# Short runs of indirect transfers, with a wait for a turned block between them, in a routed-experts kernel

## What is computed

```python
def ffn(x, router_w, w1, w2):                     # x: (4, 512, 128), 8 experts, hidden 512
    xf = x.reshape(-1, d)
    probs = softmax(xf @ router_w.T, axis=-1)
    topv, topi = top_k(probs, 2)
    topv = topv / (topv.sum(axis=-1, keepdims=True) + 1e-09)
    cw = (one_hot(topi, e) * topv[..., None]).sum(axis=1)
    h = gelu(einsum('td,edh->teh', xf, w1), approximate=False)
    y = einsum('teh,ehd->ted', h, w2)
    return einsum('te,ted->td', cw, y).reshape(b, s, d)

x = x + 0.5 * ffn(layernorm(x), router_w, w1, w2)
x = x + attention(layernorm(x), Qw, Kw, Vw)       # causal, one head of 128
x = x + 0.5 * ffn(layernorm(x), router_w, w1, w2)
```

## Time and profile before

| | |
|---|---|
| median of 3 runs | 418.84 us (416.03 to 419.93) |
| the profiled execution | 416.92 us |
| its span from first to last instruction | 415.2 us |
| PE busy with matmuls | 278.6 us, 67% of the span |
| POOL busy | 159.5 us, 38% |
| DVE and ACT busy | 152.0 us and 143.9 us |
| TensorE's mean granted clock | 0.818 of full speed |

### The profile page before, as it was taken

The page is one execution under the profiler, slowest core; times in us unless marked ns, Lnnn a source line. Parts: engine busy times, 40 slices in busy tenths (PEclk is TensorE's granted clock), DMA queues, the critical chain, the costliest instruction groups (busy, mean ns, idle before and its releaser), DMA issues.

```text
span 415.2 us, 6711 instructions
## 1 busy us (share of the span) xinstructions
PE 278.6 (67%) x1985; PEld 253.5 (61%) x1986; DVE 152.0 (37%) x675; ACT 143.9 (35%) x280; POOL 159.5 (38%) x187
## 2 busy tenths in 40 slices
PE   3226359981399359997376781599718998878650
PEld 2216359971299259985165551499618998878640
DVE  5691015710111013574169651557002221312234
ACT  4212125521154035653133241275114564434220
POOL 4447710067414720007702477001760006566650
PEclk9999559996589658999575787789856999889785
DMA  7913231122195210111100011112211222222115
GB/s 252 321 34 95 52 33 34 34 59 57 44 211 183 58 44 27 38 41 46 52 6 0 2 44 51 47 33 58 83 51 55 76 66 70 59 70 77 57 38 171
DMA packets 34254, 29.33 MB, mean 71 GB/s; under 512 B 4824, under 2 KB 29152, under 8 KB 34224
## 3 DMA queue, kind: packets, MB, share of 16 engines
q1 hardware_dynamic: 29312, 18.65, 15.0%
q0 software_dynamic: 4768, 9.78, 9.8%
q10 hardware_dynamic: 144, 0.52, 0.3%
HBM read 15.68 MB, written 13.26 MB: 70 GB/s over the span
## 4 chain that ended last, share of the span: by engine, by line
PE 51%; another core or an unknown queue 18%; issue 13%; DVE 10%; DMA 3%; ACT 2%; ACTq 1%; POOL 1%; SPq 0%; DVEq 0%; POOLq 0%
PE bank L1073 20%; PE bank L1085 18%; PE bank L1064 3%; PE bank L1143 2%; DVE xs L871 2%; PE bank L1030 2%; PE bank L1123 2%; PE bank L1014 2%; PE bank L1107 1%; PE bank L1133 1%; ACT w_block L567 1%; DVE xa L732 1%; DMA router_rows<-in_L_ffn_router_w 1%; DMA y_rows<-final_rows 1%
## 5 line engine op out<-in xcount | busy, mean ns | idle before, releaser
L1073 PE MATMUL bank<-xT,w_block 128*128 128x128 f32 x736 | 113.8, 300 | 37.8 <-issue 27.0
L1073 PEld LDWEIGHTS bank<-xT,w_block 128*128 128x128 f32 x736 | 102.8, 214 | 41.4 <-issue 36.5
L1085 PE MATMUL bank<-w_sb,act 128*128 x736 | 109.2, 296 | 19.5 <-issue 11.2
L1085 PEld LDWEIGHTS bank<-w_sb,act 128*128 128x128 f32 x736 | 100.0, 211 | 23.9 <-issue 23.9
L573 ACT ACTIVATE act<-bank 128x512 f32<-128x512 f32 x92 | 54.9, 597 | 157.8 <-PE bank L1073 72.1
L857 DVE COPY yb<-bank 128x128 f32<-128x128 f32 x92 | 26.6, 290 | 183.9 <-PE bank L1085 91.6
L500 POOL DMA_INDIRECT y_rows<-slots_out,slot_of x48 | 45.9, 957 | 64.9 <-DMA slots_out<-yb 50.9
L476 POOL DMA_INDIRECT xb_first<-xn_rows,row_in x46 | 43.6, 949 | 57.7 <-issue 42.9
L567 ACT COPY w_block<-w_sb 128x512 f32 x92 | 56.4, 613 | 20.7 <-issue 20.4
L511 POOL DMA_INDIRECT final_rows<-yb,row_of x23 | 22.4, 974 | 52.0 <-DVE row_of L847 38.2
L844 DVE COPY xT<-bank 128x128 f32<-128x128 f32 x92 | 26.1, 283 | 20.4 <-remote 13.4
(11 more groups left out here) (124 smaller groups left out, 243.5 us busy)
## 6 DMA issues: line engine op xcount, KB each, us to landing
slots_out<-yb SPq DMA_DIRECT2D x69, 64.0 KB
w_sb<-in_L_ffn_w SPq DMA_DIRECT2D x8, 512.0 KB, 7.4
xb_numbered<-numbered_slots SPq DMA_DIRECT2D x23, 64.5 KB
slots_in<-w_sb SPq DMA_DIRECT2D x4, 368.0 KB
xb_numbered<-slots_in SPq DMA_DIRECT2D x23, 64.0 KB
numbered_slots<-numbered SPq DMA_DIRECT2D x3, 387.0 KB
xs<-in_L_attn_x SPq DMA_DIRECT2D x4, 256.0 KB, 3.4
out<-xs SPq DMA_DIRECT2D x8, 128.0 KB
```

Source lines behind the costliest of these rows:

```text
L1073: mm = nc.tensor.matmul(h_ps[k][:, q * P:(q + 1) * P], w1_block[c2 % UNROLL][:, q * P:(q + 1) * P], xT[c2 % UNROLL][:], start=True, stop=True)
L1085: mm = nc.tensor.matmul(y_ps[k][:, 0:D], act[c3 % UNROLL][:, q * P:(q + 1) * P], w2_sb[:, bass.ds(at + q * D, D)], start=(q == 0), stop=(q ...
```

## The change

The kernel adds waits to POOL's program and nothing else. Blocks, banks, buffers and the programs of the other four engines stay as they are.

- `gather_in(0)`: ahead of gather b = 5, 10, 15 and 20, POOL waits until `xT_ready` is at least b-3 (2, 7, 12 and 17).
- `gather(0)`: ahead of tiles t = 2, 4 and 6, so after every fourth transfer, POOL waits until `xT_ready` is at least 33, 36 and 39.
- `scatter(3)`: ahead of tiles t = 3 and 6, so after the sixth and the twelfth transfer, POOL waits until `xT_ready` is at least 46+12 and 46+15.

```diff
+        BURST, BURST_LEAD = 5, 3
+        FIRST_RETURN_WAITS = {2: 33, 4: 36, 6: 39}
+        LAST_SCATTER_WAITS = {3: 12, 6: 15}
...
                     if g:
                         pool.wait_ge(xT_ready, b + 1)
+                    elif b and b % BURST == 0:
+                        pool.wait_ge(xT_ready, b - BURST_LEAD)
                     pool.indirect_dma_start(
                         xb_first[:, b, :], None, xn_rows[g],
...
                 for t in range(GT):
+                    if r == 3 and t in LAST_SCATTER_WAITS:
+                        pool.wait_ge(xT_ready, BLOCKS + LAST_SCATTER_WAITS[t])
                     for k in range(TOP):
                         here, rows = slots_in, xn[g][:, t, :]
...
                 for t in range(GT):
+                    if p == 0 and t in FIRST_RETURN_WAITS:
+                        pool.wait_ge(xT_ready, FIRST_RETURN_WAITS[t])
                     for k in range(TOP):
                         pool.indirect_dma_start(
                             y_rows[g][:, t, k, :], None, slots_out[g],
```

## The result

The changed kernel takes 391.75 us (median of 4 runs, 390.55 to 394.53) against 418.6 us before: a ratio of 0.9375, 95% interval 0.9308 to 0.9442, 6.3% faster. (Ratios are formed over the single executions and are not exactly the quotient of two medians.) The profiled execution took 390.55 us, with a span of 388.8 us (26.4 less). Measured again in a later group of runs, the same kernel came to a ratio of 0.9551 (0.9475 to 0.9627). The two intervals don't overlap, so the gain is 4.5 to 6.3%, and 6.3% is the better of two measurements; where the difference lies is told with the experiments.

What follows compares the result with a forecast made beforehand. PE's standstills were taken as the bound: its signals are held up while POOL issues indirect transfers in a row. Gains of 9.2, 8.6 and 3.5 us sum to 21.3, span 415.2 to 393.9, forecast 397 us, range 382 to 410.

Steps and rivals of the forecast that it cites:

- Part 1: gather_in(0): block 6 turned 13.3 us earlier, at 46.5; two runs of five then cost 2.5 us; block 16 at 70.2.
- Part 2: Unsplit gather_in(1), queued behind three gathers: a run of 22 transfers, signals 3.5 us after it; 9.2 us left (5 to 14).
- Part 3: gather(0): split into fours, it loses 9.0 us instead of 17.6, so 8.6 us gained (5 to 13).
- Part 4: scatter(3): first wait changes nothing, second holds POOL by the late count of block 14; 3.5 us gained (0 to 6).
- short runs cost almost nothing: Rival for all split stretches: signals pile up only after some six transfers, fives and fours lose nothing; 385 us, 24%.
- No gain: Rival for all split stretches: POOL's runs are not the cause or the waits are met; gain 0, 419 us, 5%.
- POOL's cover: gather_in(0): PE never lacks a block, since gather 10 lands 2.9 us after issue and is needed 7.6 us after its wait.

Runs made afterwards that it cites:

- the landing waits: Kernel before, with gather(0) in fours, POOL waiting only for the landing of its own four transfers and nothing of PE's: ratio 0.9724.
- the run with fives: Changed kernel with gather_in(1) also split, in runs of 6, 5, 5, 5 and 9, and gather(0)'s waits one step later: 395.79 us, ratio 0.94 to the kernel before.
- the plain run: Kernel before, with gather(0)'s 16 indirect transfers replaced by 16 plain ones of the same size, group 0's results not sorted back: ratio 0.9576.
- the second profile: The changed kernel itself, unaltered, measured and profiled again in a later group of runs against the kernel before: 401.03 us, ratio 0.9551.
- this part alone: Only the three waits in gather(0) kept, those in gather_in(0) and scatter(3) taken out, against the kernel before: ratio 0.9689.

## Why the prediction was right, point by point

The forecast was 397 us with a range of 382 to 410; 391.75 lies in it, and so does the 401.03 of the second measurement. The gain was forecast at 21.3 us of span and came to 26.4. None of its three terms came as forecast (9.2, 8.6 and 3.5 us; measured 6.3, 14.0 and 5.4), and the one that fell short took back part of what the others gave beyond it. That the sum came so near is in part luck.

- **The mechanism** (signals from PE are held up while POOL issues indirect transfers in a row, and a pause lets them through) is borne out as far as the pause goes, by the landing waits; that the length of a run sets the price, and not the number of pauses, has the run with fives behind it more than the table. The prediction wrote "indirect" without a row that could tell them from plain ones; the plain run bears the word out. That it is PE's signals and nothing else isn't shown. PE itself is slow beside a run: the eight matmuls of line 1073 for one block have no wait between them in the kernel and take 1.06 us when nothing disturbs them, but within the run of 20 before they stood like this:

```profile
95.20 0.62 ACT L567 COPY w_block<-w_sb 128x512 f32 x1 [0.34 <-issue]
95.92 0.81 PE L1073 MATMUL bank<-xT,w_block 128*128 128x128 f32 x5 [3.26 <-ACT w_block L567]
98.44 0.37 PE L1073 MATMUL bank<-xT,w_block 128*128 128x128 f32 x1 [1.72 <-issue]
99.84 0.37 PE L1073 MATMUL bank<-xT,w_block 128*128 128x128 f32 x1 [1.03 <-issue]
101.24 0.37 PE L1073 MATMUL bank<-xT,w_block 128*128 128x128 f32 x1 [1.02 <-issue]
```

  ACT's signal to PE took 0.1 us there (95.82 to 95.92), in the same run in which PE's to DVE took over 20. So what is slow is on PE's side, its signals and its own matmuls; which of the two comes first stays open.
- **Part 1.** Block 6 was forecast for 46.5 and came at 44.35; the two runs of five were priced at 2.5 us and cost 3.9 after, and 7.5 in the second profile. Block 16 came at 69.42 (70.2 forecast), since the two errors nearly cancel. The price of a five was too low: it came from the cheapest runs of the last stretch. The same stretch of before had a dearer one that the prediction passed over. Beside and just behind the four transfers from 347.14 to 351.97, which follow two others after a break of 0.74 us, a step takes 5.32 us in place of 1.9:

```profile
350.46 0.27 PE L1064 MATMUL bank<-ident,xb_numbered 128*128 128x128 f32 x1
...
355.78 0.32 PE L1064 MATMUL bank<-ident,xb_numbered 128*128 128x128 f32 x1 [1.25 <-issue]
```

- **Part 2.** The run of 22 was right, to its length (70.47 to 97.69). But PE turned three more blocks beside it, not four, and the count came 4.5 us after its end, not 3.5. So 6.3 us were left at block 29, not 9.2.
- **Part 3.** 14.0 us, not 8.6, beyond my own 13. The mis-sized term is the loss of the four fours: 9.0 forecast, 3.8 measured (6.2 with this part alone). I had priced the first two runs together like one of six, since the pause between them would be 0.7 us. It was 1.90 us. The turn it waited for was not late (block 29 to 32 in three clean steps, 122.32 to 128.01, and POOL went on at 128.55). But POOL had begun at 121.96, 0.4 us ahead of block 29's turn and not 0.3 behind it as before, and my end of the first four, 133.9, had the 0.3 us between two transfers in it. The second pause was 2.50 us because block 35 did come late: when a run has held PE up, the wait for a turned block is longer by that. That the longer first pause is all of the difference isn't shown.
- **Part 4.** 5.4 us (3.5 forecast), and 3.1 alone. As worked out, the first wait held nothing and the second held by the late count alone: a pause of 2.67 us after twelve, "remote".
- **The rest** (attention 0.9 us slower, the last stretch 1.6 faster) was forecast at nothing.

The ends of the three parts add up to 385 and 408 us, not to the 383 and 407 that the prediction gives; its range holds either way.

Of the rivals, "short runs cost almost nothing" (385 us) lies about as near to the 391.75 as the forecast does. It was too hopeful where fives ran (13.7 us for parts 1 and 2, 6.3 measured) and nearer than the forecast where fours did (15 and 5 for parts 3 and 4, 14.0 and 5.4 measured). "No gain" was what the prediction drew from "SBUF — State Buffer" of the Trainium skill (section "SBUF: two separate sides"), where TensorE and ScalarE wait for no one. That section speaks of the ports of SBUF. The runs decide against a forecast of no gain from it, since PE loses 17.8 us beside sixteen indirect transfers; whether any port has a part in that no run shows. Beside plain transfers PE is busy 30.34 of 30.34 us, as the section would have it. POOL's cover held: behind the start of the phase PE waited once for a gathered block, for 0.42 us.

## What to carry to other kernels

Look beside a long row of indirect transfers for "remote" waits of the other engines and for single matmuls more than a microsecond apart; that is time which no engine's busy share shows. Break the row after every fourth transfer with a wait that takes some 2 us (1.5 to 2.6 in most of the runs here), the landing of the last one if nothing else offers, provided that the consumers can stand the transfers coming later. Shorter runs than four and shorter pauses were not tried. A wait that is met when it comes breaks nothing, so look in the trace for the runs that came out. Splitting one row may join its tail to the next, so split the next one too.

## What the runs showed of the hardware

- Sixteen indirect transfers from POOL in a row cost 17.8 us of the phase beside 15.1 us of POOL's own; sixteen plain ones of the same size, 8.57 us of POOL, cost nothing.
- The cost falls when the row is broken, and the shorter the pieces the more: 3.8 to 6.2 us for four fours, 8.6 for 6, 6, 4, 14.7 for two eights. It doesn't depend on the rows per transfer (64 or 128: 48.26 and 48.12 us).
- A count raised by PE was seen by DVE and POOL some 22 us later in the row of 20, 4.5 us after the row's end in the one of 22. PE's own matmuls of one block started 1.40 us apart beside the row of 20, and a signal from ACT reached PE there in 0.1 us.
- A pause of 1.5 to 2.6 us after every fourth transfer took most of the cost away, with a wait for a turned block (34.15 and 34.41 us for the stretch) as with one for POOL's own landing (35.92).
- Why the indirect form does this isn't shown: no run took apart what POOL does in one, and no plain row as long in time as the sixteen indirect ones was tried.
